# Expert weights of a perceiver block asked for in another order: gate, value, then the down tile of the expert before

## The chip, the cores and the metric

The kernel runs on one core of one Trainium2 chip. Its time is the device time of one execution in microseconds (us), as the median of several runs.

## What is computed

The reference is one perceiver block on 512 tokens (8 batches of 64) of width 512: cross attention over a context of 512 rows for each batch, linear attention, and a mixture of 16 experts in which each expert picks its best 8 tokens of each batch, plus a shared block that all tokens pass. All of it is in float32. The part that matters here:

```
topk_w, topk_idx = jax.lax.top_k(scores, cap)          # 16 experts, cap = 8
x_tok = jnp.take_along_axis(hidden_states[:, None, :, :], topk_idx[..., None], axis=2)
g = jnp.einsum('becd,efd->becf', x_tok, Wg)            # F = 1024
u = jnp.einsum('becd,efd->becf', x_tok, Wu)
h = jax.nn.gelu(g, approximate=False) * u
eo = jnp.einsum('becf,edf->becd', h, Wd) * topk_w[..., None]
...
shared = jnp.einsum('bsf,df->bsd', jax.nn.gelu(gs, approximate=False) * us, Ws_d)
return out + shared
```

Each expert has three weights of 512 x 1024 in float32, 2048 KB each: gate (Wg), value (Wu) and down (Wd). All 48 of them are read once.

## The kernel before

The program is written engine by engine, with semaphores. The first 410 us or so are cross attention, linear attention and routing. Then comes the expert stage. Its work is a list of items, `ITEMS`: 16 experts `("e", e)`, and the shared block cut into 8 parts `("s", i)`. The order is s0, e0, e1, s1, e2, e3, s2, and so on to e10, e11, s6, e12, e13, e14, s7, e15. So a shared part stands behind each odd expert up to e11, and the last one stands between e14 and e15.

TensorE goes through the items in a software pipeline. For item n it does the gate product (`item_gate(n)`), the transposes of item n-1, the value product (`item_value(n)`), and then the down product of the item before (`item_down(n - 1)`). ScalarE and VectorE do the gelu and the product in between. For an expert, gate, value and down are sixteen matmul instructions each (L1410 for gate and value, L1447 for down). Shared parts use L1420 and L1460, with weights that are in SBUF since before the stage.

The expert weights are held twice: `w_g`, `w_u` and `w_d` have two buffers each, for even and odd experts. They are loaded by DMAs from SyncE's queue, one DMA for each tile. `expert_load(kind, e)` (L436 is its DMA) first waits until TensorE has used the tile of expert e-2 in the same buffer:

```
if e >= 2:
    n = AT["e", e - 2]
    sp.wait_ge(used, downs_upto(n) if kind == "d" else n + 1)
sp.dma_start(tiles[e % 2][:], src[e]).then_inc(arrived[e % 2], 16)
```

SyncE does its instructions strictly in order, so a load that waits holds up all loads behind it. TensorE in turn waits in `item_up` and `item_down` for `arrived` of its tile. ScalarE's queue sends finished expert rows (16 KB each, L382) to another buffer during the stage, and SyncE's queue does so for the last two experts it handles, e13 and e14, and sends the output (L454) at the end.

Of the kernel before, what the change touches and what calls it, by code (L numbers as in the profile page):

```python
# [23 lines left out]
E, CAP, FF = 16, 8, 1024  # L24
# [14 lines left out]
def perceiver_block(nc, x_d, ctx_d, wq_d, bq_d, wk_d, bk_d, wv_d, bv_d, wo_d, bo_d, wqkv_d, proj_d,  # L39
                    wout_d, bout_d, gate_d, wg_d, wu_d, wd_d, wsg_d, wsu_d, wsd_d, out_d):  # L40
    main = ExitStack()
    with main:
# [323 lines left out]
        def downs_upto(n):  # L366

            return experts_upto(n) + NT * shared_before(n + 1)
# [11 lines left out]
        def send_row(queue, e, b):  # L380
            row = SLOTS * (e % 2) + CAP * b
            queue.dma_start(eo_slot[CAP * e:CAP * (e + 1), b, :], eo_of(e)[row:row + CAP, :]).then_inc(eo_sent[e % 2], 16)  # L382
# [13 lines left out]
        @block.sync  # L396
        def _(sp):
            for dt in range(KT):
                sp.dma_start(wk_raw[:, dt], wk_d[:, dt]).then_inc(wk_in[dt], 16)
                sp.dma_start(ctx_raw[:, dt], ctx_d[0, :, dt]).then_inc(ctx0_in[dt], 16)  # L400
            for tile, src in ((bias_k, bk_d), (bias_q, bq_d), (bias_v, bv_d)):
                sp.dma_start(tile[:], src).then_inc(bias_in, 16)
            sp.dma_start(wv_raw[:], wv_d).then_inc(wv_in, 16)
            sp.dma_start(x[:], x_d.rearrange("(t p) d -> p t d", p=P)).then_inc(x_in, 16)
            sp.dma_start(wq_raw[:], wq_d).then_inc(wq_in, 16)
            sp.dma_start(bo_rows[:], bo_d.partition_broadcast(P)).then_inc(rows_in, 16)
            with sp.Fori(1, B) as b:
                sp.wait_ge(ctx_split, b + KT - 1)
                sp.dma_start(ctx_raw[:], ctx_d[b]).then_inc(ctx_in, 16)
            sp.dma_start(w_o[:], wo_d).then_inc(wo_in, 16)  # L410
            sp.dma_start(w_qkv[:], wqkv_d).then_inc(wqkv_in, 16)
            sp.wait_ge(x_done, NT)
            sp.dma_start(bout_rows[:], bout_d.partition_broadcast(P)).then_inc(rows_in, 16)
            for q in range(4):
                sp.dma_start(proj_twice[HD * q:HD * (q + 1)], proj_d[q % 2]).then_inc(proj_in, 16)
            sp.dma_start(w_out[:], wout_d).then_inc(wout_in, 16)
            sp.wait_ge(xbias_done, 2 * NT)
            sp.dma_start(gate[:], gate_d).then_inc(gate_in, 16)
            sp.wait_ge(qkv_lo_dve, KT)
            sp.wait_ge(qkv_lo_pool, 2 * KT)  # L420
            sp.dma_start(ws_g[:], wsg_d).then_inc(wsg_in, 16)
            sp.wait_ge(kv_ps, NT * KT)
            sp.dma_start(ws_u[:], wsu_d).then_inc(wsu_in, 16)
            sp.dma_start(w_u0[:], wu_d[0]).then_inc(wu_in[0], 16)
            sp.dma_start(w_d0[:], wd_d[0]).then_inc(wd_in[0], 16)
            sp.dma_start(ws_d[:], wsd_d).then_inc(wsd_in, 16)
            sp.wait_ge(att_done, 2 * NT)
            sp.dma_start(w_g0[:], wg_d[0]).then_inc(wg_in[0], 16)
            def expert_load(kind, e):

                tiles, src, arrived, used = {"g": (w_g, wg_d, wg_in, g_ps), "u": (w_u, wu_d, wu_in, u_ps),
                                             "d": (w_d, wd_d, wd_in, down_ps)}[kind]
# [5 lines that stand above are left out]
            expert_load("g", 1)  # L438
            expert_load("u", 1)
            sp.wait_ge(slot_ps, 2 * KT)  # L440
            expert_load("d", 1)
            for e in range(2, E, 2):
                for kind, ahead in (("g", 0), ("u", 0), ("g", 1)):
                    expert_load(kind, e + ahead)
                for kind, ahead in (("d", 0), ("u", 1), ("d", 1)):
                    expert_load(kind, e + ahead)
            sp.wait_ge(g_ps, AT["s", NF - 2] + 1)
            for e in range(LATE, E - 1):
                sp.wait_ge(eo_done, e + 1)
                for b in range(B if e < E - 2 else B // 2):  # L450
                    send_row(sp, e, b)
            for t in range(NT):
                sp.wait_ge(y_done, t + 1)
                sp.dma_start(out_d[P * t:P * (t + 1), :], x[:, t, :]).then_inc(out_sent, 16)  # L454
            sp.wait_ge(out_sent, 16 * NT)
# [1165 lines left out]
```

## Time and profile before

| what | value |
|---|---|
| median of 3 runs | 686.85 us (686.22 to 687.11) |
| profiled execution, its own time | 684.16 us |
| its span, first to last instruction | 682.4 us |
| TensorE matmul busy | 646.4 us, 95% of the span |
| VectorE busy | 319.7 us, 47% |
| ScalarE busy | 252.6 us, 37% |
| SyncE queue (q1), share of 16 DMA engines over the span | 47.7% |

Busy times are of one profiled execution. Matmuls are pipelined, so a busy TensorE is not one at its peak. The clock column (PEclk) gives the clock that was granted to TensorE as a part of 2.4 GHz.

### The profile page before, as it was taken

Reading aid. Unit: us, or ns where it says so; the run is one execution under the profiler, and the core shown is the slowest. Engines: PE = TensorE matmul, PEld = TensorE weight load, DVE = VectorE, ACT = ScalarE, POOL = GpSimd, SP = SyncE. Lnnn points to the kernel's source line nnn. Section 1 sums busy time; section 2 is a strip of 40 time slices with the busy share of each in tenths; the row PEclk is TensorE's granted clock in tenths of the full one; section 3 lists DMA queues with packets and bytes.
Section 4 is the critical chain, followed back from the end, with each engine's and each line's share of the span. In section 5 each row is a group of like instructions: output and inputs, shape, how many; then the busy total and the mean of one; then the engine's idle time right before and its main releaser. Section 6 shows DMA issues by size and latency. Waiting matters only on the chain.

```text
span 682.4 us, 10389 instructions
## 1 busy us (share of the span) xinstructions
PE 646.4 (95%) x4216; PEld 418.3 (61%) x4216; DVE 319.7 (47%) x654; ACT 252.6 (37%) x482; POOL 32.5 (5%) x34
## 2 busy tenths in 40 slices
PE   6989999999999999899999978999999999998897
PEld 5767777787877776478978455444443534443342
DVE  5964634446363544765778764323223231313122
ACT  4644644455453544265683342111120221121110
POOL 0300000000000000084000000000000000000000
PEclk9999999999999999989999988999999999999899
DMA  8211011010510000123038713989999999999941
GB/s 305 81 62 63 1 63 42 22 62 1 239 71 2 0 2 2 42 67 127 1 115 379 320 50 134 377 355 399 391 418 411 411 403 395 388 380 395 366 190 61
DMA packets 14347, 129.55 MB, mean 190 GB/s; under 512 B 2720, under 2 KB 2848, under 8 KB 6240
## 3 DMA queue, kind: packets, MB, share of 16 engines
q1 hardware_dynamic: 12576, 127.15, 47.7%
q10 hardware_dynamic: 1728, 1.77, 0.8%
q8 instruction: 33, 0.54, 0.3%
q14 instruction: 10, 0.08, 0.0%
HBM read 125.90 MB, written 1.05 MB: 186 GB/s over the span
## 4 chain that ended last, share of the span: by engine, by line
PE 80%; DVE 9%; DMA 5%; ACT 4%; issue 1%; SPq 1%; DVEq 0%; ACTq 0%
PE ps L1142 22%; PE ps L1410 15%; PE ps L1447 8%; PE ps L1420 6%; PE ps L1325 4%; PE ps L1212 4%; DMA w_u<-in_wu 4%; PE ps L1460 3%; PE ps L1289 3%; PE ps L1188 2%; PE ps L1223 2%; PE ps L1253 2%; PE ps L1362 2%; PE ps L1374 1%; PE ps L1436 1%
## 5 line engine op out<-in xcount | busy, mean ns | idle before, releaser
L1410 PE MATMUL ps<-w_g,x_slot 128*64 128x512 f32 x256 | 59.7, 609 | 4.3 <-DMA w_g<-in_wg 3.5
L1447 PE MATMUL ps<-w_d,hid_T 128*64 128x512 f32 x256 | 58.1, 596 | 1.4 <-ACT hid_T L712 1.4
L1410 PE MATMUL ps<-w_u,x_slot 128*64 128x512 f32 x256 | 58.1, 595 | 0.2 <-DMA w_u<-in_wu 0.2
L555 ACT ACTIVATE probs<-ps,neg_max 128x512 f32<-128x512 f32 x64 | 43.5, 688 | 39.1 <-DVE neg_max L843 39.1
L696 ACT ACTIVATE hid<-ps 128x512 f32<-128x512 f32 x24 | 14.3, 598 | 111.9 <-PE ps L1410 85.2
L823 DVE COPY probs_T<-ps 128x512 f32<-128x512 f32 x32 | 22.1, 692 | 68.7 <-PE ps L1212 68.7
L1142 PE MATMUL ps<-wv_hi,ctx_hi 128*128 128x512 f32 x128 | 51.5, 402 | 0.0
L1016 DVE TENSOR_TENSOR hid<-hid,ps 128x512 f32<-128x512 f32 x24 | 16.5, 687 | 73.1 <-PE ps L1410 42.9
L1142 PE MATMUL ps<-wv_lo,ctx_hi 128*128 128x512 f32 x128 | 50.0, 390 | 0.0
L1142 PE MATMUL ps<-wv_hi,ctx_lo 128*128 128x512 f32 x128 | 49.8, 389 | 0.0
L843 DVE TENSOR_REDUCE neg_max<-ps 128x1 f32<-128x512 f32 x64 | 39.7, 682 | 18.4 <-PE ps L1188 18.3
L1142 PE MATMUL ps<-ctx_hi,wk_hi 128*128 128x512 f32 x112 | 44.4, 397 | 0.4 <-ACT k_T L540 0.4
L1142 PE MATMUL ps<-ctx_hi,wk_lo 128*128 128x512 f32 x112 | 43.6, 390 | 0.0
L1142 PE MATMUL ps<-ctx_lo,wk_hi 128*128 128x512 f32 x112 | 43.6, 389 | 0.0
L1410 PEld LDWEIGHTS ps<-w_g,x_slot 128*64 128x64 f32 x256 | 18.1, 140 | 40.3 <-issue 35.0
L1447 PEld LDWEIGHTS ps<-w_d,hid_T 128*64 128x64 f32 x256 | 17.6, 137 | 36.4 <-issue 33.9
L540 ACT ACTIVATE k_T<-ps,bias_k 128x512 f32<-128x512 f32 x32 | 21.6, 690 | 48.8 <-PE ps L1142 48.8
L1410 PEld LDWEIGHTS ps<-w_u,x_slot 128*64 128x64 f32 x256 | 17.9, 137 | 33.4 <-issue 32.9
L725 ACT COPY x_slot<-ps 64x512 f32<-64x512 f32 x14 | 8.1, 580 | 77.6 <-PE ps L1447 77.6
L1142 PEld LDWEIGHTS ps<-wv_hi,ctx_hi 128*128 128x128 f32 x128 | 24.0, 188 | 15.9 <-issue 5.7
L836 DVE TENSOR_SCALAR probs<-probs,row_inv 128x512 f32<-128x512 f32 x64 | 31.2, 487 | 2.3
L1212 PE MATMUL ps<-ident,probs 128*128 128x128 f32 x256 | 31.0, 274 | 0.0
(237 smaller groups left out, 1197.1 us busy)
## 6 DMA issues: line engine op xcount, KB each, us to landing
w_u<-in_wu SPq DMA_DIRECT2D x16, 2048.0 KB, 15.6
w_d<-in_wd SPq DMA_DIRECT2D x16, 2048.0 KB, 11.9
w_g<-in_wg SPq DMA_DIRECT2D x16, 2048.0 KB, 12.8
ctx_raw<-in_ctx SPq DMA_DIRECT2D x7, 1024.0 KB, 4.8
w_qkv<-in_wqkv SPq DMA_DIRECT2D x1, 3072.0 KB, 15.1
ws_g<-in_wsg SPq DMA_DIRECT2D x1, 2048.0 KB, 7.8
ws_u<-in_wsu SPq DMA_DIRECT2D x1, 2048.0 KB, 7.8
ws_d<-in_wsd SPq DMA_DIRECT2D x1, 2048.0 KB, 21.2
```

The costliest lines, as they stand in the source:

```text
L540: act.activation(k_T[:, ht, :], bank(FIRST_K + ht if first else PROJ[ht % 2]), ACT.Identity, bias=bias_k[:, ht:ht + 1], scale=1.0).then_in ...
L555: act.activation(probs[:, p, :], bank(SCORE[p]), ACT.Exp, bias=neg_max[:, p:p + 1], scale=1.0, accum_out=row_sum[:, p:p + 1]).then_inc(exp ...
L823: dve.tensor_copy(probs_T[:, ht % 2, 1].rearrange("p s c -> p (s c)"), bank(TRANS[ht % 2][1])).then_inc(pT_done[1], 1)
L836: dve.tensor_scalar(probs[:, p, :], probs[:, p, :], row_inv[:, p:p + 1], None, ALU.mult).then_inc(prob_done, 1)
L843: dve.tensor_reduce(neg_max[:, p:p + 1], bank(SCORE[p]), AX.X, ALU.max, negate=True).then_inc(max_done, 1)
L1142: ins = pe.matmul(dst, a(dt), c(dt), start=(dt == 0 and i == 0), stop=(dt == KT - 1 and i == 2))
L1212: ins = pe.transpose(ps[:, TRANS[ht % 2][pr], P * st:P * (st + 1)], probs[:, 2 * ht + pr, P * st:P * (st + 1)], ident[:])
L1289: ins = pe.matmul(bank(RES_BANK[k] + t), rows_T[:, dt, P * t:P * (t + 1)], w[:, dt, :], start=(dt == 0), stop=(dt == KT - 1))
L1325: ins = pe.matmul(bank(qkv_bank(n)), a, c, start=(dt == 0 and i == 0), stop=(dt == KT - 1 and i == 2))
L1410: ins = pe.matmul(ps[64 * fh:64 * (fh + 1), dst, :], x_slot[:, e, dt, :], weights[e % 2][:, dt, BANK * fh:BANK * (fh + 1)], start=(dt == 0 ...
L1420: ins = pe.matmul(bank(dst), a, c[:, dt, :], start=(dt == 0 and j == 0), stop=(dt == KT - 1 and j == 2))
L1447: ins = pe.matmul(ps[64 * fh:64 * (fh + 1), 6 + n % 2, :], hid_T[:, n % 2, j, 64 * fh:64 * (fh + 1)], w_d[e % 2][:, KT * fh + j, :], start ...
```

## The change

The order in which SyncE asks for the weights of experts 2 to 15 is another. The loads themselves, their waits and their buffers are the same, and the other engines' programs are not touched.

```diff
             sp.wait_ge(slot_ps, 2 * KT)
             expert_load("d", 1)
-            for e in range(2, E, 2):
-                for kind, ahead in (("g", 0), ("u", 0), ("g", 1)):
-                    expert_load(kind, e + ahead)
-                for kind, ahead in (("d", 0), ("u", 1), ("d", 1)):
-                    expert_load(kind, e + ahead)
+            for e in range(2, E):
+                expert_load("g", e)
+                expert_load("u", e)
+                if e > 2:
+                    expert_load("d", e - 1)
+            expert_load("d", E - 1)
             sp.wait_ge(g_ps, AT["s", NF - 2] + 1)
```

Here is SyncE's queue at the start of the loop. The number behind a tile's name is its buffer (0 for even experts, 1 for odd ones). The first two rows are u2 and g3, and the last three that are kept or added are u4, d3 and g5:

```order
 L436 DMA w_u0<-in_wu 128x4096 [waits u_ps]
 L436 DMA w_g1<-in_wg 128x4096 [waits g_ps]
+L436 DMA w_u1<-in_wu 128x4096 [waits u_ps]
 L436 DMA w_d0<-in_wd 128x4096 [waits down_ps]
-L436 DMA w_u1<-in_wu 128x4096 [waits u_ps]
-L436 DMA w_d1<-in_wd 128x4096 [waits down_ps]
 L436 DMA w_g0<-in_wg 128x4096 [waits g_ps]
 L436 DMA w_u0<-in_wu 128x4096 [waits u_ps]
+L436 DMA w_d1<-in_wd 128x4096 [waits down_ps]
 L436 DMA w_g1<-in_wg 128x4096 [waits g_ps]
```

The value tile u3 moves ahead of d2, and the down tile d3 moves behind g4 and u4.

And here is the same queue at the end of the loop. The first row is u13 where it now stands, then come d12, u13 and d13 where they stood, then g14, u14, d13, g15, u15, d14, u15 (where it stood) and d15:

```order
+L436 DMA w_u1<-in_wu 128x4096 [waits u_ps]
 L436 DMA w_d0<-in_wd 128x4096 [waits down_ps]
-L436 DMA w_u1<-in_wu 128x4096 [waits u_ps]
-L436 DMA w_d1<-in_wd 128x4096 [waits down_ps]
 L436 DMA w_g0<-in_wg 128x4096 [waits g_ps]
 L436 DMA w_u0<-in_wu 128x4096 [waits u_ps]
+L436 DMA w_d1<-in_wd 128x4096 [waits down_ps]
 L436 DMA w_g1<-in_wg 128x4096 [waits g_ps]
+L436 DMA w_u1<-in_wu 128x4096 [waits u_ps]
 L436 DMA w_d0<-in_wd 128x4096 [waits down_ps]
-L436 DMA w_u1<-in_wu 128x4096 [waits u_ps]
 L436 DMA w_d1<-in_wd 128x4096 [waits down_ps]
```

The down tile d13 moves behind g14 and u14, and u15 moves ahead of d14. TensorE's order, which is the same in both, is here: gate 14, value 14, down 13, shared part 7 (gate and value), down 14, gate 15, value 15, down of shared part 7, and at the end down 15.

## Rows read from the trace of the kernel before

**Rows 1.** The page: busy tenths and GB/s in 40 slices of the span.

```profile
PE   6989999999999999899999978999999999998897
DMA  8211011010510000123038713989999999999941
GB/s 305 81 62 63 1 63 42 22 62 1 239 71 2 0 2 2 42 67 127 1 115 379 320 50 134 377 355 399 391 418 411 411 403 395 388 380 395 366 190 61
```

**Rows 2.** Chain of waits, in order of time: start us, us, what, and how many.

```profile
604.36 3.58 PE ps L1447 x16
607.94 6.89 PE ps L1410 x32
614.85 24.47 DMA w_u<-in_wu
...
639.36 3.65 PE ps L1410 x16
...
646.45 2.98 PE ps L1420 x12
...
652.64 3.58 PE ps L1447 x16
```

**Rows 3.** Timeline of TensorE, 626 to 640: start us, us, engine, instructions [idle before].

```profile
626.18 3.65 PE L1447 MATMUL ps<-w_d,hid_T 128*64 128x512 f32 x16 [0.68 <-ACT hid_T L712]
633.31 5.27 PE L1410 MATMUL ps<-w_g,x_slot 128*64 128x512 f32 x16 [3.48 <-DMA w_g<-in_wg]
```

**Rows 4.** Windows of the expert stage: us, busy of each engine, PEclk, DMA share, GB/s.

```profile
454.00:456.00 2.00, 2.00 (x12) 0.66 (x10) 0.69 (x1) 0.56 (x1) 0.00 (x0) 1.00 0.67 147
453.90:484.70 30.80, 30.80 (x144) 14.04 (x142) 8.70 (x13) 5.97 (x11) 0.00 (x0) 1.00 0.97 386
577.10:607.90 30.80, 30.80 (x144) 14.04 (x142) 8.70 (x13) 5.97 (x11) 0.00 (x0) 1.00 1.01 383
607.90:646.50 38.60, 34.25 (x151) 11.96 (x148) 8.61 (x13) 6.06 (x12) 0.00 (x0) 0.96 1.00 384
633.30:637.00 3.70, 3.69 (x10) 1.13 (x12) 0.00 (x0) 0.00 (x0) 0.00 (x0) 0.55 1.00 359
```

**Rows 5.** Timeline of SyncE's queue: start us, us, queue, line and the DMA issued.

```profile
441.28 0.33 SPq L436 DMA_DIRECT2D w_d<-in_wd  x1
441.66 0.43 SPq L436 DMA_DIRECT2D w_u<-in_wu  x1
453.98 0.33 SPq L436 DMA_DIRECT2D w_d<-in_wd  x1
457.41 0.33 SPq L436 DMA_DIRECT2D w_g<-in_wg  x1
...
584.04 0.33 SPq L436 DMA_DIRECT2D w_u<-in_wu  x1
...
607.98 0.33 SPq L436 DMA_DIRECT2D w_d<-in_wd  x1
...
630.25 0.43 SPq L436 DMA_DIRECT2D w_u<-in_wu  x1
646.49 0.33 SPq L436 DMA_DIRECT2D w_d<-in_wd  x1
```

**Rows 6.** DMAs issued at 441.66, 453.98, 584.04, 607.98, 630.25, 646.49: last column, us to landing.

```profile
w_u<-in_wu SPq DMA_DIRECT2D x1, 2048.0 KB, 14.1
w_d<-in_wd SPq DMA_DIRECT2D x1, 2048.0 KB, 8.0
...
w_u<-in_wu SPq DMA_DIRECT2D x1, 2048.0 KB, 20.4
...
w_d<-in_wd SPq DMA_DIRECT2D x1, 2048.0 KB, 19.3
...
w_u<-in_wu SPq DMA_DIRECT2D x1, 2048.0 KB, 24.9
...
w_d<-in_wd SPq DMA_DIRECT2D x1, 2048.0 KB, 13.9
```

## The prediction, made before the result was known

> **What bounds the kernel now.** I first read the slices of the page: TensorE is busy in nearly every slice, and from about slice 27 on the DMA engines are full too [rows 1]. The expert stage therefore has two limits close together, and the question is which of them ends last, and where. The chain of waits answers it [rows 2]. It runs through TensorE's matmuls all along the stage but for one link: the value weights of expert 14, asked for at 614.85, are on the chain for 24.47 us. The rows of TensorE at that place [rows 3] show the stall before it: 3.48 us without work until the gate weights of expert 14 land, and then sixteen half matmuls that take 5.27 us where the same sixteen take 3.65 us elsewhere. The window of those matmuls has a granted clock of 0.55, near 1.2 GHz, while the windows of full rounds have 1.00, that is 2.4 GHz [rows 4].
>
> The windows give the cause of the late weights. One round (two experts and one shared block) takes TensorE 30.8 us, and loads six tiles of 2048 KB, 12.6 MB, which is 408 GB/s. The DMA share is 0.97 in the round from 453.9, 1.01 in the one from 577.1 and 1.00 in the one from 607.9, and these three move 383 to 386 GB/s [rows 4]; the slices between go up to 418 [rows 1]. Over the whole stage the loads so fall behind the matmuls. The issues and the times to landing tell the same: 8.0 us for the down tile asked for at 453.98, 20.4 us for the value tile of 584.04, 24.9 us for the value tile of 630.25 [rows 5, 6]. It is one queue that grows. It first hurts at expert 14, because no shared block stands between experts 13 and 14: gate 14 comes right behind down 12. I write g, u and d for the three loads of an expert.
>
> **The change, part by part.** No byte, no load and no matmul is added or removed. Two things move: when SyncE asks, and which tile holds which place in the queue.
>
> *Which place.* The n-th tile of a full queue lands when n tiles have been moved, whatever their names. Before, the six of a round are d(odd) g u g d u; now they are g u d(odd) g u d. So g14 takes the place that d13 had, u14 that of g14, d13 that of u14, g15 keeps its place, u15 takes that of d14, and d14 that of u15. Each odd down tile goes back by two places. The order that is asked for now is not quite that of use: TensorE wants d(e) of an odd expert ahead of the next even expert's gate (the shared block lies between), and in the last round it wants d14 ahead of g15, since shared block 7 stands between experts 14 and 15.
>
> *When it is asked (the lag).* d(odd) now stands behind u of the next expert. At the start of the stage the queue is still short, and this leaves it empty: before, u3 asked for at 441.66 lands 14.1 us later, at 455.8, and d3 asked for at 453.98 lands at 462.0 [rows 5, 6]. Before, the DMA share had a dip already at 454 to 456 (0.67) [rows 4]. Now u3 stands ahead of d2, which TensorE frees at 441.28, so both are asked for by then. Both land by 455.8 at the latest, and the next request is g4 at 457.41. With the 8.0 us of d3, a tile that found the queue empty, g4 lands at 465.4. That is the same number of tiles, 3.4 us later. Against that stands what idle time the queue had after this place and will not have when it is fuller: 0.97 of 30.8 us leaves 0.9 us, of which 0.7 us lies in the window 454 to 456, so 0.2 to 0.3 us. I take a lag of **3.1 us**. Its bounds are 3.4 us (nothing made good) and 0 (the slower share of the DMA engines had work all through). From then on the queue is never empty in this forecast, so the lag stays to the end.
>
> *What TensorE meets.* Places from before, plus 3.1:
> - d11 has the place of u12 (584.04 + 20.4 = 604.4), so it lands at 607.5. Down 11 began at 604.36 [rows 2]: TensorE waits 3.2 us that it did not wait before.
> - g14 has the place of d13 (607.98 + 19.3 = 627.3): 630.4. Before, TensorE was free for it at 629.83 (633.31 less 3.48), now at 633.0, so it does not wait there. The stall of before is gone.
> - u14 has the place of g14 (633.3): 636.4. Gate 14 ends at 636.6, and value 14 starts some 0.6 us later, after four transposes. No wait. It ends at about 640.7.
> - d13 has the place of u14 (639.3): 642.4, so TensorE waits 1.7 us, and down 13 ends at 646.0. Before it ended at 646.45. Here the change is 0.4 us ahead: what the two gate and value tiles gained, d13 has paid.
> - d14 has the place of u15 (630.25 + 24.9 = 655.2): **658.3**. Shared block 7 runs before it, 6.2 us (646.45 to 652.64), so TensorE is there at 652.2 and waits 6.1 us. Against the 652.64 of before this is 5.6 us late [rows 2].
>
> What is hidden: the loads g15, u15 and d15 (before at 660.4, 13.9 us after 646.49, now 663.5) are wanted behind down 14, so not before 662, and cost nothing. The row sends and the output behind them on SyncE wait for TensorE's results, and move with it.
>
> *The clock.* A wait of 6.1 us is longer than that of 3.48 us which left TensorE at 0.55 of its clock for one 3.7 us window [rows 4]. That cost 5.27 - 3.65 = 1.6 us [rows 3]. After it nothing waits for DMA any more, so it stays on the path. I take **1.6 us** once; its bounds are 0 and twice that. The lower clock that the waits for d11 and d13 may bring is absorbed by the wait behind them.
>
> Sum: 5.6 + 1.6 = **+7.2 us** on a span of 682.4 us, which is 689.6 us. The profiled execution took 684.16 us, 2.7 us under the median of 686.85 us of the runs shown; the same difference on the median gives **694.0 us**, 1.0% slower.
>
> A page bears on the rate. The Trainium skill, "DMA: Bandwidth & Descriptors", section "Where 436 GB/s comes from", puts the ceiling at 435 GB/s. By that a tile would take 4.8 us and six of them 28.9 us, less than a round, and the queue would not grow. The trace disagrees, with 383 to 386 GB/s at a share of 0.97 to 1.01 [rows 4] and 418 in the best slice [rows 1].
>
> **The rivals.**
> - *The queue keeps up in this order (faster).* If a tile took no more than 5.1 us (30.8 / 6), d14 would land long before 652.6 and g14 before 629.8. All DMA waits would go: 3.48 + 1.6 + 0.2 us, and the time is about 681.5. For it: tiles asked for early land some 5 us apart. Against it: landings from 462.0 to 655.2 are 35 tiles in 193.2 us, 5.5 us each. The point from which it decides: d14 just meets TensorE at 5.35 us each, 3% quicker than now. Chance 0.05.
> - *The waits move but cancel (no change).* d14 lands within about 1 us of 652.6. That needs no lag, and 2.5 us found elsewhere in the queue, by the same 3% or less. It gives 686 to 688. Chance 0.05.
> - *The lag is not carried.* If the gap at 457 is filled from a backlog of the slowest DMA engines, d14 lands at 655.2, 2.5 us late, and with the clock +4.1 us: 691.0. For it: the share of the rows is a mean over 16 engines, and landing is that of the last one. Against it: 8.0 us for d3 shows that the queue was really empty. Chance 0.13.
> - *The late waits cost more.* A second stretch at half clock (+1.6) and a queue 1% slower over the 193 us (+1.9), with the whole lag of 3.4 (+0.3): +11.0 us, 697.9. Chance 0.07.
> - The forecast, 694.0, with 1.5 us either way for lag and clock: chance 0.70.
>
> **How the numbers follow.** The range holds the forecast and the two slower-side neighbours in part: from 689.4 (no lag and no clock loss, +2.5) to 697.9 (+11.0). Some 0.1 lies below it and 0.05 above. A measurement of this kernel can tell about 0.2% (1.4 us) from no change. Faster by more than that: 0.05; within it: 0.05; slower: 0.90.
>
> **What would show it.** In the profile after: SyncE asks for d3 at about 461 and for g4 at 457.4, and the DMA share has a hole at 454 to 458; the wait for the gate tile of expert 14 is gone; TensorE waits for w_d three times, about 3, 2 and 6 us, at about 604, 641 and 652, the last ending at about 658; a stretch at half clock follows it; the chain of waits goes through w_d instead of w_u. It is wrong if the tiles come less than 5.35 us apart, if the hole does not shift later landings, or if down 14 starts before 654.

## The result, and the profile after

The changed kernel took 691.66 us (median of 8 runs, 688.88 to 693.64) where the one before took 685.39 us (median of 8 runs, the three of the table above among them, 679.93 to 687.11). The ratio is 1.0093, with a 95% interval from 1.0069 to 1.0118: 0.9% slower. The forecast was 694.0 us, 1.0% slower, with a range from 689.4 to 697.9 us. The profiled execution has a span of 690.8 us.

The page of the changed kernel, in the same slices as [rows 1] (each is a little longer now, as the span is):

```profile
PE   6989999999999999799998889999999999989787
DMA  8111011010600000303057806969999999999921
GB/s 304 78 62 62 1 63 61 2 62 2 280 25 2 1 1 2 96 12 125 1 216 287 351 0 267 419 229 426 393 417 398 409 399 399 386 366 388 365 84 61
```

Slice 27 fell to 229 GB/s, where slices 26 to 28 moved 377, 355 and 399 GB/s before [rows 1]. That is the hole in the queue. The chain of waits goes through the down tiles now, where it went through the value tile of expert 14 before [rows 2]:

```profile
584.14 23.30 DMA w_d<-in_wd
607.58 5.35 PE ps L1448 x16
...
631.14 3.68 PE ps L1448 x16
634.84 23.85 DMA w_d<-in_wd
658.82 5.85 PE ps L1448 x16
664.67 6.87 PE ps L1411 x32
```

The timeline of TensorE at down 11, down 13 and down 14 (L1448 is the line that was L1447), to be set beside [rows 3]:

```profile
607.58 5.35 PE L1448 MATMUL ps<-w_d,hid_T 128*64 128x512 f32 x16 [3.46 <-DMA w_d<-in_wd]
...
642.23 3.60 PE L1448 MATMUL ps<-w_d,hid_T 128*64 128x512 f32 x16
...
658.82 5.85 PE L1448 MATMUL ps<-w_d,hid_T 128*64 128x512 f32 x16 [6.77 <-DMA w_d<-in_wd]
```

The wait for g14 is gone. There are waits of 3.46 us for d11 and of 6.77 us for d14, and the sixteen half matmuls behind each take 5.35 and 5.85 us instead of 3.65. Windows of the changed kernel, with the columns of [rows 4]; the last one is that of down 14:

```profile
454.00:456.00 2.00, 2.00 (x12) 0.61 (x10) 0.69 (x1) 0.18 (x1) 0.00 (x0) 1.00 0.00 0
453.90:484.70 30.80, 30.80 (x144) 14.04 (x142) 8.70 (x13) 5.97 (x12) 0.00 (x0) 1.00 0.88 355
577.10:607.90 30.80, 27.34 (x126) 13.31 (x124) 8.71 (x13) 5.79 (x11) 0.00 (x0) 1.00 1.01 387
658.80:664.50 5.70, 5.68 (x17) 1.92 (x19) 0.00 (x0) 0.00 (x0) 0.00 (x0) 0.61 0.31 121
```

Between 454 and 456 no DMA engine had work; before, their share there was 0.67. The round from 453.9 has 0.88 instead of 0.97, which is 2.8 us less of work for the queue. SyncE's queue and the landings at both ends of the stage, to be set beside [rows 5, 6]:

```profile
457.03 0.33 SPq L436 DMA_DIRECT2D w_g<-in_wg  x1
460.46 0.33 SPq L436 DMA_DIRECT2D w_u<-in_wu  x1
460.83 0.44 SPq L436 DMA_DIRECT2D w_d<-in_wd  x1
```

The first of these landed after 8.3 us, the down tile asked for at 634.84 (d14) after 23.9 us:

```profile
w_g<-in_wg SPq DMA_DIRECT2D x1, 2048.0 KB, 8.3
...
w_d<-in_wd SPq DMA_DIRECT2D x1, 2048.0 KB, 23.9
```

So g4 landed at 465.4 and d14 at 658.7.

**A common clock for all runs.** The work ahead of the experts shifts the stage from one execution to the next, by up to 3.9 us among the profiles here. To compare profiles, I count from the request for g3 (TensorE has done gate 1). It is at 433.68 before and 433.30 after, and this is down 14 of the kernel before:

```profile
433.68 0.33 SPq L436 DMA_DIRECT2D w_g<-in_wg  x1
...
652.57 3.65 PE L1447 MATMUL ps<-w_d,hid_T 128*64 128x512 f32 x16
...
433.30 0.33 SPq L436 DMA_DIRECT2D w_g<-in_wg  x1
```

"Stage" below is the time from that request to the end of the span: 248.7 us before and 257.5 us after, 8.8 us more. "Lag" is how much later the n-th tile of the stage landed than the n-th tile before, whatever their names. In the change, the lag was 3.7 us at the place where g4 now stands, 2.5 to 4.5 us from there up to that of u14 (where d13 now stands), and 3.9 us at that of u15, where d14 now stands.

### The profile page after: what moved, and what is told of

It reads as the page before. It is cut to its first block, busy times and chain, and to the rows that moved or that the text cites. A ratio compares the mean times of both kernels' runs of the same rounds, so it can differ in the third digit from the quotient of the medians.

```text
span 690.8 us, 10389 instructions
## 1 busy us (share of the span) xinstructions
PE 647.2 (94%) x4216; PEld 420.0 (61%) x4216; DVE 320.9 (46%) x654; ACT 252.7 (37%) x482; POOL 32.5 (5%) x34
## 4 chain that ended last, share of the span: by engine, by line
PE 75%; DVE 9%; DMA 8%; ACT 4%; ACTq 2%; issue 2%; SPq 1%; DVEq 0%
PE ps L1143 22%; PE ps L1411 13%; PE ps L1448 8%; DMA w_d<-in_wd 7%; PE ps L1326 4%; PE ps L1213 4%; PE ps L1421 4%; PE ps L1290 3%; PE ps L1461 3%; PE ps L1189 2%; PE ps L1224 2%; PE ps L1254 2%; PE ps L1363 2%; ACTq L382 2%; PE ps L1375 1%
## 5 line engine op out<-in xcount | busy, mean ns | idle before, releaser
L1448 PE MATMUL ps<-w_d,hid_T 128*64 128x512 f32 x256 | 62.0, 629 | 11.6 <-DMA w_d<-in_wd 10.2
L1411 PE MATMUL ps<-w_g,x_slot 128*64 128x512 f32 x256 | 58.1, 595 | 0.8 <-ACT x_slot L732 0.8
L1448 PEld LDWEIGHTS ps<-w_d,hid_T 128*64 128x64 f32 x256 | 19.2, 144 | 49.1 <-issue 46.6
L1040 DVE TENSOR_TENSOR x_slot<-ps,x_slot 64x512 f32<-64x512 f32 x14 | 9.6, 688 | 49.5 <-ACT x_slot L726 49.5
```

The lines of the kernel that those rows point to most:

```text
L1411: ins = pe.matmul(ps[64 * fh:64 * (fh + 1), dst, :], x_slot[:, e, dt, :], weights[e % 2][:, dt, BANK * fh:BANK * (fh + 1)], start=(dt == 0 ...
L1448: ins = pe.matmul(ps[64 * fh:64 * (fh + 1), 6 + n % 2, :], hid_T[:, n % 2, j, 64 * fh:64 * (fh + 1)], w_d[e % 2][:, KT * fh + j, :], start ...
```

## The experiments

All of them change the order of requests only, unless the text says otherwise. Lags and stages come from one profile of each kernel, and they scatter too. In kernels whose order is that of before up to some tile, the landings ahead of it came up to 2.0 us later than before's. So a lag under about 2 us is not told from scatter here.

**One load late.** The order of before, but d3 behind g4 and u4:

```diff
-            for e in range(2, E, 2):
+            for kind, e in (("g", 2), ("u", 2), ("g", 3), ("d", 2), ("u", 3),
+                            ("g", 4), ("u", 4), ("d", 3), ("g", 5), ("d", 4), ("u", 5), ("d", 5)):
+                expert_load(kind, e)
+            for e in range(6, E, 2):
```

> The order of before, with one load moved: d3 behind g4 and u4. My theory (the hole in the queue at 457 is carried to the end as a lag of about 3 us): g4 lands at about 465.4, every later tile about 3 us later than before, g14 at about 636.4 instead of 633.3, and the kernel is 3 to 4 us slower (ratio 1.004 to 1.006). Rival (the lag is made good within a few rounds, because the slowest DMA engines had a backlog): g14 lands at 633 to 634 and the time is that of before.

Measured: 686.87 us, ratio 1.0031 (1.0017 to 1.0044). The chain of waits of this run, which goes through g14 as before:

```profile
612.55 25.55 DMA w_g<-in_wg
638.14 5.24 PE ps L1413 x16
```

TensorE waits 3.30 us for u13 and 4.70 us for g14, where it waited 3.48 us for g14 before. The lag is 3.8 us at g4 and never goes: 2.5 to 4.3 us at all places from there to that of u14, 32 tiles later. The stage is 252.1 us, 3.4 us more than before, but the timed ratio says less: 2.1 us on 684.58 us (1.2 to 3.0), under the 1.004 to 1.006 that I expected. One request 3.4 us later, some 180 us ahead of the wait for g14, shows at the end, as 2.1 us in the timed runs and 3.4 us of stage. The rival "the lag is not carried" is out: the landings stay late, and the time is above that of before.

**The hole undone, first try.** The order of the change, but d3 ahead of g4:

```diff
             for e in range(2, E):
+                if e == 4:
+                    expert_load("d", 3)
                 expert_load("g", e)
                 expert_load("u", e)
-                if e > 2:
+                if e > 2 and e != 4:
                     expert_load("d", e - 1)
```

> The order of the change, but d3 still ahead of g4 and u4, so that the queue has no hole at 457. My theory: no lag, d14 in the place of u15 lands at about 655.2, down 14 starts about 2.5 us late, with a stretch at half clock behind it (1.6 to 2.2 us): 4 to 5 us slower than before (ratio 1.006 to 1.007), 3 us faster than the change. Rival (places alone make the loss): down 14 starts at 658 to 659 as in the change, ratio 1.009.

Measured: 693.31 us, ratio 1.0117 (1.0094 to 1.0141), no faster than the change. My expectation was wrong, and two windows of this run tell why (the same windows have a share of 0.73 and 0.98 before):

```profile
452.00:458.00 6.00, 6.00 (x30) 2.01 (x28) 0.69 (x1) 0.58 (x1) 0.00 (x0) 1.00 0.48 147
...
484.70:489.00 4.30, 4.30 (x22) 1.44 (x20) 0.69 (x1) 0.76 (x2) 0.00 (x0) 1.00 0.33 131
```

The hole has moved by one round, to d5. The lag is 0.2 us at g5, 1.8 at g6 and 2.7 at d5, and stays at 2.4 to 3.7 us up to the place of u14. So the edit did not take away what it was meant to.

**The hole undone, second and third try.** The order of before up to u7 (d7 is the first to go back), and the same up to u11 (d11 is the first). The second of them:

```diff
-            for e in range(2, E, 2):
-                for kind, ahead in (("g", 0), ("u", 0), ("g", 1)):
-                    expert_load(kind, e + ahead)
-                for kind, ahead in (("d", 0), ("u", 1), ("d", 1)):
-                    expert_load(kind, e + ahead)
+            for e in range(2, 12, 2):
+                for kind, ahead in (("g", 0), ("u", 0), ("g", 1), ("d", 0), ("u", 1), ("d", 1)):
+                    if (kind, e + ahead) != ("d", 11):
+                        expert_load(kind, e + ahead)
+            for e in range(12, E):
+                expert_load("g", e)
+                expert_load("u", e)
+                expert_load("d", e - 1)
+            expert_load("d", E - 1)
```

> The order of before up to u7, and from there that of the change (d7 is the first down tile that goes behind the next gate and value). Keeping d3 alone only put off the hole: there d5 went back while the queue was still short, and 8.0 us lay between two landings at 489 to 497. At g8 (asked for at 519 before, with 13.1 us to landing) the queue is long enough, so my theory is: no hole, tiles at most 0.5 us later than in the order of before, d14 lands about 3 us sooner than in the change, and the kernel is 4 to 5.5 us slower than before (ratio 1.006 to 1.008). Rival (the hole is not what makes the lag; places alone or a queue that is slower in this order do): down 14 starts as late as in the change, ratio 1.009 or more.

> The order of before up to u11, then that of the change: only d11, d13 and d14 go back. With d7 as the first one the tiles still came 1.5 to 2 us late, with a DMA share of 0.97 in that round, so the queue was not yet long enough. At g12 before, 18.2 us lie between request and landing. My theory: now really no lag, tiles at the places of before within 0.7 us up to d13; no wait for d11; no wait for g14; down 13 waits about 2 us; d14 lands at about 655 to 656 in the time of before and down 14 starts 3 us late, with a stretch at half clock: 4 to 5.5 us slower than before (ratio 1.006 to 1.008). Rival (there is a loss in this order that neither places nor lag make): 6 us or more, ratio 1.009.

Measured, from d7 on: 692.68 us, ratio 1.0107 (1.0079 to 1.0135). From d11 on: 689.62 us, ratio 1.0078 (1.0054 to 1.0101). With d7 the time was that of the rival (1.009 or more), and the lag was still 1.3 to 2.2 us for most of the way and 2.6 to 2.9 us at the last places: this window of it has a share of 0.97 where the round before it has 1.00.

```profile
515.50:546.30 30.80, 30.80 (x143) 14.04 (x141) 8.70 (x14) 5.97 (x11) 0.00 (x0) 1.00 0.97 386
```

So the expectation of "at most 0.5 us" for the lag was wrong. I had read the queue's length from g8's 13.1 us, but d7, which no longer stands ahead of g8, was 5.5 us of them. The lag is 0.8 us at g8 and 1.9 us at u8. With d11 the lag is below 0.6 us from g6 up to the place of u14, and 0.7 us at that of u15. TensorE's timeline there:

```profile
637.85 3.65 PE L1451 MATMUL ps<-w_d,hid_T 128*64 128x512 f32 x16 [1.86 <-DMA w_d<-in_wd]
...
654.56 5.87 PE L1451 MATMUL ps<-w_d,hid_T 128*64 128x512 f32 x16 [6.87 <-DMA w_d<-in_wd]
```

No wait for d11, 1.86 us for d13, 6.87 us for d14. On the common clock down 14 starts 3.5 us later than before, and the stage is 254.4 us, 5.7 us more. With the lag and the places together (the change) it is 8.8 us. The intervals of the timed runs of d3 kept, d7, d11 and the change overlap, so the 3 us that the lag is worth here are told by the profiles and by the run with one load late, not by these ratios. The parts do add up. The lag alone cost 3.4 us of stage and the places alone 5.7 us, 9.1 us together, against 8.8 us in the change; in timed runs it is 2.1 and 5.2 us, against 6.3 us.

**The place of d14 alone.** The change, with d14 ahead of g15 and u15:

```diff
             for e in range(2, E):
+                if e == E - 1:
+                    expert_load("d", e - 1)
                 expert_load("g", e)
                 expert_load("u", e)
-                if e > 2:
+                if 2 < e < E - 1:
                     expert_load("d", e - 1)
```

> The order of the change, but d14 is asked for ahead of g15 and u15. My theory (only the last wait, for d14, is a loss; the waits for d11 and d13 are paid by the stall that is gone): d14 has the place of g15 and lands at about 647.8, before TensorE comes to it at about 652; no wait for d14, no stretch at half clock behind it, and the time is within 1 us of before (ratio 0.998 to 1.002). Rival (the wait for d11 and the lag cost by themselves): the 3.5 us at down 11 and its half clock stay on the path, 3 to 5 us slower than before (ratio 1.004 to 1.007).

Measured: 684.3 us, ratio 0.9991 (0.9974 to 1.0009). The timeline of TensorE:

```profile
652.51 3.65 PE L1450 MATMUL ps<-w_d,hid_T 128*64 128x512 f32 x16
...
667.66 3.65 PE L1567 MATMUL ps<-eo_slot,give 120*64 120x512 f32 x16 [1.58 <-DMA eo_slot<-eo]
```

Down 14 has no wait and starts, on the common clock, 0.2 us later than before, in spite of a wait of 3.49 us for d11 and a lag of 2.6 to 4.4 us up to the place of u14. One request put ahead of two others takes back the whole loss. What is left in the profile (stage 250.7 us, 2.0 us more) came behind it: u15 and d15 landed 4.4 and 4.7 us later than in the kernel before, the last rows of ScalarE and SyncE stand behind them, and TensorE waits 1.58 us for these rows.

**The place of d13 alone, from before.** The order of before, with d13 behind g14 and u14:

```diff
-            for e in range(2, E, 2):
+            for e in range(2, E - 2, 2):
                 for kind, ahead in (("g", 0), ("u", 0), ("g", 1)):
                     expert_load(kind, e + ahead)
                 for kind, ahead in (("d", 0), ("u", 1), ("d", 1)):
-                    expert_load(kind, e + ahead)
+                    if (kind, e + ahead) != ("d", E - 3):
+                        expert_load(kind, e + ahead)
+            for kind, e in (("g", E - 2), ("u", E - 2), ("d", E - 3), ("g", E - 1),
+                            ("d", E - 2), ("u", E - 1), ("d", E - 1)):
+                expert_load(kind, e)
```

> The order of before, with one load moved: d13 behind g14 and u14, all else as before. My theory: g14 has the place of d13 and lands at about 627.3, u14 at 633.3, d13 at 639.4; no wait for g14, a wait of about 1.7 us for d13, none or 1 us for d14 (650.2): 2 to 3 us faster than before (ratio 0.995 to 0.997). Rival (bringing gate and value forward is worth the whole stall with its half clock): 5 us faster, ratio 0.992; rival (the queue just hands the stall on): no change.

Measured: 682.45 us, ratio 0.997 (0.9955 to 0.9986). The timeline:

```profile
638.73 5.35 PE L1451 MATMUL ps<-w_d,hid_T 128*64 128x512 f32 x16 [2.50 <-DMA w_d<-in_wd]
```

There is no wait for g14, and 2.50 us for d13, with a granted clock of 0.57 behind it. There are also waits of 1.47 us for u13 and 0.76 us for u14, which I had not expected. In the timed runs this kernel takes 2.1 us less than before. In this one profile the stage is 249.0 us, as before. The landings were late in this execution: 2.0 us behind before's at d12, where the order is still that of before, and up to 2.6 us at g15.

**The wait filled with work.** The change, with 27 matmuls ahead of TensorE's wait for d14:

```diff
+                    if e == E - 2:
+                        for _ in range(27):
+                            pe.matmul(bank(3), ws_g_hi[:, 0, :], xn_hi[:, 0, :], start=True, stop=True)
                     pe.wait_ge(wd_in[e % 2], 16 * (e // 2 + 1))
```

> The change, with 27 more matmuls (128x512, about 0.23 us each, 6.2 us in all) on TensorE ahead of its wait for d14; they write a bank that nobody reads before it is written anew, so the result is the same. They fill the wait for d14 of 6.8 us. My theory: no stretch at half clock behind the wait, down 14 takes 3.65 instead of 5.85 us, and the kernel is about 2 us faster than the change (4 to 5 us slower than before, ratio 1.006 to 1.007). Rival (the slow matmuls behind the wait come from the full DMA or from something else at that place): still 5 us or more for down 14, ratio 1.009. If the extra matmuls are longer than the wait, they delay down 14 by what they are longer.

Measured: 688.96 us, ratio 1.0079 (1.005 to 1.0107). The timeline:

```profile
650.59 6.48 PE L1447 MATMUL ps<-xn_hi,ws_g_hi 128*128 128x512 f32 x27
657.01 3.65 PE L1451 MATMUL ps<-w_d,hid_T 128*64 128x512 f32 x16
```

Down 14 takes 3.65 us where it took 5.85, and starts at the same time on the common clock (225.4 and 225.5 us). The stage is 255.2 us, 2.3 us less than in the change. That is the price of the clock alone. The timed ratio is a little above the 1.006 to 1.007 that I expected, and its interval overlaps the change's.

**The order of use in every round.** g, u, g, u, d, d; and in the last round g14, u14, d13, d14, g15, u15, d15. Then the same with g15 ahead of d14, and the last round alone with the earlier ones as before. The first of the three, against before:

```diff
-            for e in range(2, E, 2):
-                for kind, ahead in (("g", 0), ("u", 0), ("g", 1)):
-                    expert_load(kind, e + ahead)
-                for kind, ahead in (("d", 0), ("u", 1), ("d", 1)):
-                    expert_load(kind, e + ahead)
+            for e in range(2, E - 2, 2):
+                for kind, ahead in (("g", 0), ("u", 0), ("g", 1), ("u", 1), ("d", 0), ("d", 1)):
+                    if (kind, e + ahead) != ("d", E - 3):
+                        expert_load(kind, e + ahead)
+            for kind, e in (("g", E - 2), ("u", E - 2), ("d", E - 3), ("d", E - 2), ("g", E - 1),
+                            ("u", E - 1), ("d", E - 1)):
+                expert_load(kind, e)
```

> The true order of use in every round: g, u of the even expert, g, u of the odd one, d of both; in the last round g14, u14, d13, d14, g15, u15, d15. My theory: no hole at 457 (d3 keeps its place ahead of g4), g14 in the place of d13 at 627 to 629, u14 at 633 to 635, d13 at 639 to 641, d14 with no wait: 2 to 4 us faster than before (ratio 0.994 to 0.997), at least as fast as with d13 alone behind u14. Rival (the later request for g15, held up on SyncE by the wait of d14 for down 12, makes a new hole and a wait for g15): no gain over before.

> The order of before up to u13, and in the last round g14, u14, d13, d14, g15, u15, d15. With the true order of use in every round the time was 0.9925 of before, more than the 2 to 4 us that the last round should bring by its places. If the gain lies in the last round alone, as I think, this kernel has it too: ratio 0.992 to 0.996. Rival (the earlier rounds of the order of use give part of it): 0.996 to 0.998, as with d13 alone behind u14.

> As with the order of use in every round, but g15 ahead of d14 in the last one, so that its request isn't held up by the wait for down 12. Together with three runs there are (d13 alone behind u14: 0.997; the last round alone: 0.998; the order of use in every round: 0.9925) it makes a square: rounds before the last in the order of before or of use, and d14 behind or ahead of g15. My theory (the places before the last round are worth nothing, and 0.9925 was scatter between executions): 0.996 to 0.999. Rival (the order of use in the earlier rounds gives some 3 us by itself): 0.991 to 0.994.

Measured: 679.78 us, ratio 0.9925 (0.9901 to 0.995), for the order of use; 684.01 us, ratio 0.9983 (0.996 to 1.0007), for the last round alone; 682.03 us, ratio 0.9963 (0.9943 to 0.9983), for g15 ahead of d14. The stages are 248.0, 246.4 and 248.3 us, where before has 248.7. The run with d13 alone behind u14 has 0.997 and a stage of 249.0 us. Three of these four intervals lie below 1. The order of use did better than the 0.994 to 0.997 that I expected, and the last round alone worse than 0.992 to 0.996. The one profile of the order of use is of the slowest of its seven runs (683.19 us; the others took 679.55 to 680.72), so its stage says little of the 0.9925.

No wait for g14 or g15 is in any of these profiles. TensorE waits for d13, 1.98, 1.67 and 1.03 us in the three orders of this part, and in the last of them also 2.20 us for d14.

What the order of use gives in the rounds before the last is not settled. With g15 ahead of d14 the ratio is 0.997 without it and 0.9963 with it. With d14 ahead of g15 it is 0.9983 and 0.9925, whose intervals do not overlap.

**What makes the queue fall behind.** The change, and before, without the 104 row sends of ScalarE's queue; the products that read the rows read x instead, so the experts' part of the output is left out:

```diff
-                if 1 < n < LAST:
-                    send(n)
...
-                pe.wait_ge(eo_sent[par], 16 * B * ((E - par) // 2))
+                pe.wait_ge(eo_sent[par], 16 * B)
...
-                pe.matmul(ps[rows, Y_BANK[b // 2], :], give[0:sent, b, :], eo_slot[0:sent, b, :], start=True, stop=False,
+                pe.matmul(ps[rows, Y_BANK[b // 2], :], give[0:sent, b, :], x[0:sent, b // 2, :], start=True, stop=False,
```

> The order of the change, without the 104 row sends (16 KB each) of ScalarE's queue for experts 0 to 12; the sum of the experts' outputs reads x in place of the rows, so that part of the output is left out. It asks what makes the queue of loads fall behind. My theory: the sends take 1 to 4% of the DMA engines' time in the stage, a tile takes about 5.3 instead of 5.5 us, d14 lands 4 to 6 us sooner, the wait for d11 is gone and that for d14 under 2 us: 4 to 8 us faster than the change, about the time of before or less (ratio 0.992 to 1.001). Rival (the loads are bound by HBM or the fabric, and the sends are too small to matter): tiles as far apart as before, ratio 1.006 or more.

> The order of before without the 104 row sends of ScalarE's queue (the rows are replaced by x as in the run on the change, so that part of the output is left out). In the order of the change tiles then came 4.9 us apart and every DMA wait was gone. My theory: here too, 4.9 us apart and no wait for g14, 4 to 6 us faster than before, and the same time as the order of the change without sends within 1.5 us (ratio 0.989 to 0.994): the order is only worth something because the sends slow the loads. Rival (the sends cost through ScalarE, not through the queue): the stall at gate 14 stays.

Measured: 678.1 us, ratio 0.9895 (0.9862 to 0.9927), in the order of the change; 676.56 us, ratio 0.9889 (0.9864 to 0.9913), in that of before. I had expected 0.992 to 1.001 and 5.3 us a tile for the first. Neither has a wait for a weight tile, and down 14 starts at the same time in both on the common clock (212.4 us behind the request for g3, which is at 434.12 and 432.04), where before it was 218.9 us:

```profile
646.54 3.65 PE L1446 MATMUL ps<-w_d,hid_T 128*64 128x512 f32 x16
...
644.47 3.65 PE L1445 MATMUL ps<-w_d,hid_T 128*64 128x512 f32 x16
```

Not all of this is the loads'. The wait of 0.68 us for ScalarE ahead of down 12 [rows 3] is gone too: the sends also kept ScalarE busy. The queues of the round 577.1 to 607.9, first the changed kernel:

```profile
q1 hardware_dynamic: 789, 11.55, 97.1%
q10 hardware_dynamic: 343, 0.35, 3.4%
```

and the same without the sends:

```profile
q1 hardware_dynamic: 856, 12.47, 97.4%
```

Without the sends, in the order of the change, u14, d13, g15, u15 and d14 each land 4.9 us behind the tile before them; in the changed kernel it is 6.1, 6.0, 6.1, 6.0 and 5.1 us. Over 26 tiles from the middle of the stage it is 5.1 us a tile without (503.8 to 636.5), the 30.8 us of a round divided by six, and 5.6 with (503.0 to 647.6). Both orders take the same within their intervals.

## Why the prediction was right

**The time alone does not tell.** 691.66 us lies nearer the 691.0 us of the rival "the lag is not carried" than the forecast of 694.0 us. Both were counted from a median of 686.85 us, and the eight runs before have 685.39 us. The difference, +6.3 us, is nearer the forecast's +7.2 than that rival's +4.1. What tells the two apart is the landings and the run with one load late.

**The bound and the places: right.** d14 was forecast at 658.3 and landed at 658.7 (659.1 on the common clock). d11 was to cost 3.2 us of wait and cost 3.46. The wait for g14 went, as forecast, and nothing after down 14 waited for weights. The run with d14 ahead and the one with d13 behind show the two places apart: the first takes back all the loss, the second gives 2.1 us.

**The lag: right in size for most of the way, too simple in what removes it.** 3.1 us was forecast, from 8.0 us of latency at an empty queue. The change has 2.5 to 4.5 us, and the run with d3 alone 2.5 to 4.3 us. At d14 it was 3.9 us, above the upper bound of 3.4 us. It was still 2.6 us at d13 and grew behind it: the next tile, g15, took 6.1 us, with 76 packets of row sends beside it, and 5.4 us before, with 30. What I had not seen is that the hole isn't bound to d3. Any down tile that goes back while the queue is short opens it again, at d5 and, as far as a lag so near the scatter tells, in part at d7; with d11 as the first one, the lag was below 0.6 us.

**The waits between: one was wrong, without consequence.** For d13 I forecast a wait of 1.7 us; there was none. The tile landed at 641.5, 0.9 us sooner than forecast, and TensorE came to down 13 at 642.23, later than the forecast 640.7, as the half clock behind d11's wait (5.35 instead of 3.65 us) held it back. As forecast, this was absorbed by the wait for d14.

**The clock: right in kind, small in size.** I took 1.6 us from the matmuls behind the wait of 3.48 us [rows 3]; behind 6.77 us it was 5.85 - 3.65 = 2.2 us, and filling the wait with matmuls took away just this. The price is not a matter of the wait's length alone: behind the waits of 7.00 and 7.10 us with d7 and d3 kept it was 1.4 and 2.0 us, behind 1.98 us in the order of use 1.7 us, and behind 3.30 us with one load late it was nothing.

**The sum.** Forecast +7.2 us; the medians differ by 6.3 us, and the profiles by 8.8 us on the common clock. Most of the 2.5 us between these two is scatter: the profiled execution before was 1.2 us faster than its median, and the one after 1.0 us slower. Down 14's start, 6.6 us later there (658.82 against 652.57, and 0.38 for the clock), and 2.2 us for the half clock make up those 8.8 us. Down 14's start was forecast 5.6 us late, 1 us too little. Of this 0.8 us is the lag at d14, 3.9 and not 3.1 us. The clock's term was 0.6 us too small. In the run with the lag gone the stage loses a third less (5.7 us).

**The rivals.** "The lag is not carried" is refuted by the run with one load late. "The queue keeps up" did not happen, but its condition, at most 5.1 us a tile, is met in the kernels without the sends: there a full queue hands over a tile each 4.9 us, and the order costs nothing. An estimate from the ceiling of 435 GB/s in the Trainium skill ("DMA: Bandwidth & Descriptors", section "Where 436 GB/s comes from"), 4.8 us a tile, agrees with these 4.9 us. In the kernels that send rows, only the tiles with few sends beside them come that close.

## What to carry to other kernels

In a full queue a request that moves back moves the ones that it lets pass forward, so write down for each tile its place, its landing and the time at which it is wanted; the order of use has to be read from the consumer's program, item by item, since one extra item between two experts turned it round here. A queue that runs empty once, even 150 us ahead of the first wait, is late by that much for as long as it is full. And look at who else uses the DMA engines before tuning the order of a queue that can't keep up: here the small sends were worth more than any order.

## What the runs showed of the hardware

The row sends move 0.35 of the 11.9 MB of the round from 577.1, or 3%, and take 3.4% of the DMA engines' time there. Without them the last tiles come 4.9 us apart instead of some 6.0 us. In the round from 577.1 itself it is about 5.7 us a tile in the change. So the loads take some 16% longer where the profile shows 3.4% for the sends themselves, four to five times as much. Each send is 8 rows of 2 KB.

The changed kernel shows the same within itself. Here are its queues between the landings of d3 and g5 (476.33 to 481.24, no send packet), and between those of d13 and g15 (641.52 to 647.63):

```profile
q1 hardware_dynamic: 144, 2.10, 100.4%
...
q1 hardware_dynamic: 147, 2.15, 95.9%
q10 hardware_dynamic: 76, 0.08, 3.9%
```

The engines are full in both stretches. But a packet of the loads takes 0.55 us on average in the first and 0.64 us in the second (the share of 16 engines' time, divided by the packets). So the time is not lost in idle engines that wait for the slowest one: the packets of the loads themselves take longer beside the sends. Why they do is open.

The second thing is how long a hole lives. In the run with one load late, the mean DMA share is 1.01 in each of the four rounds behind the hole (385 to 415 GB/s), and the lag at their end is what it was at their start. There was no spare rate to make it good.
